# Six-layer decoder block on one core: GpSimd adds inputs and biases, VectorE makes some scan scalings, TensorE adds products of zeros

## What is computed

```
x = ln(x + L0_attn(x))    # hyena: x@w_in+b, short convolution, v*s1, long convolution, *s0, @w_out + b_out
x = ln(x + L0_xattn(x))   # softmax(x ctx^T/sqrt(d)) ctx (77 keys), its own layernorm * gamma + beta
x = ln(x + L0_ffn(x))     # quantised linear 128->512, gelu, quantised linear 512->128, + b2
x = ln(x + L1_attn(x))    # selective state-space scan, 256 channels, 16 states
x = ln(x + L1_xattn(x))   # 16-head cross attention with q/k norms, 77 keys, @Wo + bo
x = ln(x + L1_ffn(x))     # product-key mixture of 1024 experts, top 8 of 8 heads
```

## Time and profile before

| | us |
|---|---|
| median of 3 runs | 1079.09 |
| lowest, highest | 1075.49, 1084.47 |
| profiled execution, its own time | 1088.42 |
| its span, first to last instruction | 1086.6 |

### The profile page before, as it was taken

The page is one execution under the profiler, slowest core; times in us unless marked ns, Lnnn a source line. Parts: engine busy times, 40 slices in busy tenths (PEclk is TensorE's granted clock), DMA queues, the critical chain, the costliest instruction groups (busy, mean ns, idle before and its releaser), DMA issues.

```text
span 1086.6 us, 13799 instructions
## 1 busy us (share of the span) xinstructions
PE 816.7 (75%) x4536; PEld 591.9 (54%) x4536; DVE 768.4 (71%) x1635; ACT 697.3 (64%) x2068; POOL 298.3 (27%) x175
## 2 busy tenths in 40 slices
PE   1769485677898788988786775766688889988882
PEld 1547244566565546566555454455556664565562
DVE  1167845777755558899989677657865556999994
ACT  1423559997667665896754357678665777796660
POOL 3021102776455401000011213437554541000000
PEclk9888696988989888999999786789988999989997
DMA  8200001221100000000100001122210000000000
GB/s 239 60 1 2 0 25 49 78 78 59 49 1 1 1 0 1 18 1 1 27 1 10 1 22 30 40 60 76 71 39 1 0 1 1 1 1 1 1 1 21
DMA packets 27250, 29.06 MB, mean 27 GB/s; under 512 B 7220, under 2 KB 17194, under 8 KB 27178
## 3 DMA queue, kind: packets, MB, share of 16 engines
q1 hardware_dynamic: 25208, 26.20, 8.3%
q10 hardware_dynamic: 1970, 1.97, 0.6%
HBM read 26.33 MB, written 1.84 MB: 26 GB/s over the span
## 4 chain that ended last, share of the span: by engine, by line
DVE 35%; PE 30%; ACT 17%; issue 6%; POOL 6%; DMA 1%; POOLq 0%; DVEq 0%; ACTq 0%
DVE mem L1786 10%; ACT mem L1310 7%; POOL mem L1846 5%; DVE mem L1610 5%; DVE mem L1769 5%; ACT mem L1354 4%; PE ps L879 2%; PE ps L984 2%; PE ps L932 2%; PE ps L1105 2%; PE ps L1058 2%; DVE x L1414 2%; PE ps L846 2%; PE ps L888 1%; PE ps L1007 1%
## 5 line engine op out<-in xcount | busy, mean ns | idle before, releaser
L1826 POOL TENSOR_TENSOR rs<-ve,minus_half 128x4 f32<-128x4 f32 (+1 forms) x56 | 88.5, 1580 | 536.0 <-DVE ve L1407 422.2
L1610 DVE TENSOR_TENSOR_SCAN mem<-mem,ps 128x1024 f32<-128x1024 f32 x64 | 145.2, 2281 | 65.1 <-PE ps L879 64.8
L1846 POOL TENSOR_TENSOR mem<-mem 128x1024 f32<-128x1024 f32 x64 | 151.7, 2379 | 141.8 <-DVE mem L1610 129.0
L1105 PE MATMUL ps<-ident,mem 128*128 128x128 f32 x1024 | 140.6, 288 | 42.3 <-DVE mem L1786 37.8
L1786 DVE SCALAR_TENSOR_TENSOR mem<-mem 128x1024 f32<-128x1024 f32 x128 | 161.0, 1281 | 14.3 <-ACT mem L1354 11.8
L1354 ACT ACTIVATE mem<-mem 128x32 f32<-128x32 f32 x768 | 167.0, 314 | 3.7 <-PE ps L1105 3.7
L1105 PEld LDWEIGHTS ps<-ident,mem 128*128 128x128 f32 x1024 | 119.1, 148 | 82.5 <-DVE mem L1786 65.1
L1136 ACT ACTIVATE mem<-ps 128x1024 f32<-128x1024 f32 (+6 forms) x128 | 94.1, 748 | 108.2 <-PE ps L1058 52.5
L1310 ACT ACTIVATE mem<-ps,mem,rs 128x77 f32<-128x77 f32 x256 | 102.3, 437 | 45.3 <-DVE mem L1663 45.3
L1240 ACT ACTIVATE mem<-mem,m_A 128x511 f32<-128x511 f32 x128 | 84.1, 711 | 48.6 <-DVE mem L1610 46.6
L879 PE MATMUL ps<-ident,mem 128*128 128x128 f32 x512 | 79.3, 307 | 42.8 <-DVE mem L1610 26.4
(11 more groups left out here) (237 smaller groups left out, 1331.1 us busy)
## 6 DMA issues: line engine op xcount, KB each, us to landing
mem<-bc_rows SPq DMA_DIRECT2D x64, 256.0 KB, 3.3
mem<-in_x_dram SPq DMA_DIRECT2D x4, 256.0 KB, 3.0
mem<-key_rows SPq DMA_DIRECT2D x2, 512.0 KB
out_dram<-x SPq DMA_DIRECT2D x4, 256.0 KB, 2.3
mem<-in_mask_BxSxS_ik_dram SPq DMA_DIRECT2D x4, 154.0 KB, 3.1
mem<-n_L_ffn_expert_down_dram SPq DMA_DIRECT2D x1, 512.0 KB
mem<-in_L_xattn_Wo_dram SPq DMA_DIRECT2D x1, 512.0 KB
mem<-in_L_xattn_Wv_dram ACTq DMA_DIRECT2D x1, 512.0 KB
```

The costliest lines, as they stand in the source:

```text
L1105: mm = pe.matmul(ps[:, e // 4, (e % 4) * P:(e % 4 + 1) * P], WH[s][:, (k * PH + h) % WB, e * P:(e + 1) * P], ident[:], start=(h == 0 and e ...
L1610: nc.vector.tensor_tensor_scan((HS, TU)[n % 2][s][:].rearrange(flat), dA[s][:, n % 2].rearrange(flat), dbu.rearrange(flat), 0.0, ALU.mult, ...
L1846: nc.gpsimd.tensor_tensor(HC[s][:, n % 2], (HS, TU)[n % 2][s][:], spread(CQ[s][:, n % 2, :], 1, DJ), ALU.mult)\
```

## The change

- GpSimd gets four new additions per sample (`biased`): `R = input + bias` for `hyena`, `cross0`, `bitffn` and `cross1`. `added` becomes one float32 product of `ident` with `R`; in `cross0` and `bitffn` it goes altogether, with ScalarE's copy to `R2`, and VectorE reads `R` instead.
- In the scan VectorE makes `DZ` of four of the sixteen states of a lane (`VE_STATES`) as one `tensor_tensor` of 1024 elements (`DUT` times the spread column of `BT`), and ScalarE leaves those out.
- State 0's `DZ` is scaled straight out of PSUM; `DU` is transposed into banks 0 and 1 instead of 2 and 3; softplus' `Exp` and `Ln` come ahead of the copies of B and C, for both of which TensorE now waits.
- `zeros_added`: two bfloat16 products of a zero matrix with 512 columns are added onto bank 0 after the `DZ` transposes of each state from 2 on, and onto bank 3 after the scores of units 1 to 6 of the second cross attention. They change no sum.
- All five strings of `LANE_RUNS` are new. They start with lane 1.

```diff
+    VE_STATES = [(2, 6, 10, 14), (4, 8, 12, 15)]
...
-                def added(to, of, bias):
-                    pe.matmul(to, ident[:], of[:].rearrange("p k d -> p (k d)"), start=True, stop=False,
+                def added(s, to, turn_of):
+                    w.reach(G("xb_ready", s), turn_of)
+                    pe.matmul(to, ident[:], R[s][:].rearrange("p k d -> p (k d)"), start=True, stop=False,
                               skip_group_check=True)
-                    return pe.matmul(to, ident[:], spread(bias[:], 1, NB), start=False, stop=False,
-                                     skip_group_check=True)
+                def zeros_added(to, times, start=False):
+                    width = to.shape[1] // P
+                    for _ in range(times):
+                        pe.matmul(to, zeros_bf[:], spread(ident_bf[:], 1, width), start=start, stop=False,
+                                  skip_group_check=True)
...  (cross0, bitffn on TensorE)
-                    yield 3.1
-                    added(ps[:, 2, :], X[s], beta).then_inc(G("o_ready", s), 1)
-                    yield 4.5
-                    w.next(G("qT_ready", s), 2)
-                    added(ps[:, 1, :], X[s], b2).then_inc(G("v_ready", s), 1)
                     yield 5
-                    w.next(G("qT_ready", s), NB - 2)
+                    w.next(G("qT_ready", s), NB)
...  (scan on TensorE)
-                    w.next(G("bc_sb", s))
+                    w.next(G("bc_sb", s), 2)
-                            mm = pe.transpose(ps[:, 2 + k // 2, at:at + P], DU[s][:, j, k * P:(k + 1) * P], ident[:])
+                            mm = pe.transpose(ps[:, k // 2, at:at + P], DU[s][:, j, k * P:(k + 1) * P], ident[:])
...
                             mm.then_inc(G("dbu_done", s), 1)
+                            if n >= 2:
+                                zeros_added(ps[:, 0, :], 2)
                         if n >= 1:
                             yield (4.2, 4.8)[s] + n
+                            if n == 1:
+                                w.next(G("xT_ready", s))
...  (cross1 on TensorE)
+                        if 0 < u < 2 * NB - 1:
+                            zeros_added(ps[:, 3, :], 2)
-                    added(ps[:, 3, :], X[s], a_bo)
+                    added(s, ps[:, 3, :], 4)
...  (scan on ScalarE; Exp and Ln moved ahead of the two copies)
-                            turned(s, DUT[s][:].rearrange("p (a b) c -> p a (b c)", a=2), ps[:, 2:4, :], "xT_ready")
+                            w.next(G("turned", s))
+                            w.next(G("bc_sb", s), 2)
+                            for k in range(NB):
+                                ins = nc.scalar.activation(DZ[s][:, 0, k, :], ps[:, k // 2, k % 2 * DI:(k % 2 + 1) * DI],
+                                                           ACT.Identity, scale=BT[s][:, k, 0:1])
+                            ins.then_inc(G("dz_ready", s), 1)
+                            yield 3.5
+                            copy(DUT[s][:].rearrange("p (a b) c -> p a (b c)", a=2), ps[:, 0:2, :], G("xT_ready", s))
                             w.reach(G("xT_ready", s), XT_TURNS)
-                            w.next(G("bc_sb", s), 2)
+                            continue
+                        if n in VE_STATES[s]:
+                            continue
...  (scan on VectorE, after the recurrence of state n)
+                        if n + 2 in VE_STATES[s]:
+                            yield 4.3 + n
+                            w.reach(G("xT_ready", s), XT_TURNS)
+                            nc.vector.tensor_tensor(DZ[s][:, n % 2], DUT[s][:], spread(BT[s][:, :, n + 2], 2, DI),
+                                                    ALU.mult).then_inc(G("dzv_ready", s), 1)
...  (GpSimd)
+                def biased(s, of, bias):
+                    nc.gpsimd.tensor_tensor(R[s][:], of[:], spread(bias[:], 1, NB), ALU.add)\
+                        .then_inc(sg["xb_ready"][s], 1)
...
+                    yield 4000.2
+                    w.reach(sg["x_ready"][s], 4)
+                    biased(s, X[s], a_bo)
```

More of the change, by code:

```diff
@@ L1194, in bitffn @@
                                ps[:, k, :].bitcast(BF16)[:, 0:F], "qT_ready")
-                    yield 4.6
-                    w.reach(G("v_ready", s), len(GROUPS) + 1)
-                    copy(R2[s][:].rearrange("p k d -> p (k d)"), ps[:, 1, :], G("v_sb", s))
                 def scan(s, b):
@@ L1828, in rsqrt, with stages @@
                         .then_inc(sg["rstd_ready"][s], 1)
-                def stages(s):
-                    for stage in (4, 1003, 1004, 2000, 2003, 2005):
+                def biased(s, of, bias):
+                    nc.gpsimd.tensor_tensor(R[s][:], of[:], spread(bias[:], 1, NB), ALU.add)\
+                        .then_inc(sg["xb_ready"][s], 1)
+                def stages(s, b):
+                    yield 0.2
+                    if b >= 1:
+                        w.reach(sg["x_ready"][s], 0)
+                    w.next(sg["x_loaded"][s], 16)
+                    pool.wait_ge(p_late, ALL_LATE)
+                    biased(s, XI[s], b_out)
+                    yield 4
+                    rsqrt(s, P, NB)
+                    yield 4.6
+                    w.reach(sg["x_ready"][s], 1)
+                    biased(s, X[s], beta)
+                    for stage in (1003, 1004, 2000):
                         if stage == 1003:
@@ L1837, in stages @@
                                                     minus_half[0:C, 0:H], ALU.pow).then_inc(sg["krstd_ready"][s], 1)
+                        yield stage
+                        rsqrt(s, P, NB)
+                    yield 2000.1
+                    w.reach(sg["x_ready"][s], 2)
+                    biased(s, X[s], b2)
+                    for stage in (2003, 2005):
                         yield stage
@@ L1868, in program @@
                         w.batch(sg, TURNS, s, b)
-                        for stage in stages(s):
+                        for stage in stages(s, b):
                             yield PASS * b + clock(int(stage // 1000), stage % 1000)
```

57 lines of the change are left out of this document (31 added, 26 removed), and 39 rows, old and new, of tables (scalar, tensor, vector).

## The result

The changed kernel takes 1046.17 us, the median of 4 runs (1043.1 to 1047.16); the kernel before, run in turn with it, takes 1081.78. The ratio is 0.967 with an interval of [0.962, 0.973]: 35.6 us faster, where the prediction said 25 (1054 us, range 1016 to 1088). The profiled execution took 1047.16 us with a span of 1045.3. The same kernel was run once more beside later experiments.

The account below looks back on a forecast made before the run. No engine was full; the limit changed by stage, with ScalarE setting the pace where both lanes scan. Terms -9 - 3 - 3 + 0 - 10 = -25 took the median 1079 to 1054 us, range 1016 to 1088.

Parts of the forecast that it names:

- Scalings, -9: Where both lanes scan: moving scalings to VectorE brings 48 states from 3.03 to 2.85 us each, -9 us.
- Start of the scan, -3: State 0 no longer waits for the copy to `DUT`, and softplus starts earlier: -3 us (0 to -8).
- Additions, -3: Additions moved to GpSimd: `bitffn` gains 6 us, GpSimd's extra work costs 3, together -3 us (-6 to +13).
- The +3 for GpSimd: GpSimd's 16 additions stand ahead of reciprocal square roots and keep VectorE's two-input operations out: +3 us, from 0 to 19.
- Zeros, 0: Zero products in scans and cross attention: TensorE time costs +11 us, higher clock wins it back, 0 together (+11 to -20).
- The fourth rival: Zeros change no clock: +11 in place of 0, 1065 us; its chance lies inside the main forecast's 0.48.
- The third: Rival: zeros hold TensorE at 2.4 GHz, -18 in place of 0, 1036 us; chance 0.18 including larger gains of the strings.
- Strings, -10: New order runs the lanes closer: cover lost in pass 1, time won where a lane was alone; -10 us (-30 to +24).
- -35: Cross attention: five units a pass that ran alone save 3.5 us each, in two passes, -35 us.
- +24: Pass 1's first sublayers lose cover: VectorE's idle 20 of 114 us becomes pass 0's 44 of 124, +24 us.
- Closer lanes bringing nothing: Rival: lost cover costs 24 us, only 15 of 35 is won, +9 in place of -10, 1073 us; chance 0.20.
- The shared way to SBUF: Rival, scans: VectorE's idle time stays and each scaling adds 3.12 us, +37 in place of -9, 1100 us; chance 0.14.

Follow-up runs that it names:

- order-only kernel: The kernel before with only the five strings of `LANE_RUNS` replaced by the new ones: 1065.49 us against 1083.4, ratio 0.986 [0.981, 0.990].

## Why the prediction was right, and where its terms were off

The sign, the size class and the likeliest case were right: faster by 35.6 us, 25 forecast. The terms were less right than their sum: those of the strings and of the additions were too small by 8 and 5 us, and two of the others too large.

- **Scalings, -9.** The mechanism was right: ScalarE no longer leads, and recurrences came closer than said, 2.76 and 2.60 us apart instead of 2.85. Two parts of this term were mis-sized in the same direction: the scaling itself (1.53 instead of 1.7) and, above all, the waits between four engines near 2.6, which the forecast put at 0.25 a state and which were nearly nothing in pass 1. But the step from 3.03 was not all the scalings' doing: 2.86 to 2.92 came from the order alone. What the scalings brought is 8.7 us in the scans of the profiled executions and about 1 us, not told apart from 0, in the medians. That the -9 meets the 8.7 is chance: a greater drop a state than forecast, of which the order had a third to a half.
- **Start of the scan, -3.** 0.8 measured in the medians, not told apart from 0; in the profiled executions 3.3 in the scan of pass 0 and nothing in that of pass 1. That the other lane hides it there, the lower end that the term left open, is likely and not shown.
- **Additions, -3.** Measured -8. The -6 for `bitffn` held (2.7 and 1.0 us on the two lanes in pass 0). The +3 for GpSimd did not appear: its additions start when `x` is written, mostly on an idle GpSimd, and the square root behind one in pass 0 (101.17 us, changed kernel run again) came after 2.0 us of idle time. The rest, some 3 us, would be the products of the other sublayers, taken at 0; that is a difference and nothing shows it directly.
- **Zeros, 0.** The granted clock in the scans rose to 0.94 and 0.95, above the 0.93 named as the sign, and in the medians the net is within 3 us of nothing in the new order. The fourth rival (no change of the clock) fell. The third (-18 in place of 0) did not come either: zeros made scans and cross attentions some 7 us shorter, and longer experts took it back. The Trainium skill ("TensorE: Matmul & The Clock Gate", Part 4) says that transposes do not count as activity for the clock; the scans with no zeros ran only 27 of 143.9 and 20 of 139.5 us at the lower level. In the order-only kernel, all 339 TensorE products from 694.3 to 757.3 us are transposes, and the granted clock is 0.95. So this case doesn't bear it out; only that added zeros shortened the time at the lower level speaks for it.
- **Strings, -10.** This is the step that failed most. Measured: -18 in the medians and -22.9 in the profiled executions. By stage in the table: -11.4 and -4.1 in the scans, which the prediction had put to the scalings or nowhere; -23.3 and +6.8 in cross attention, -16.5 together where it said -35; +6.3 and +1.4 where it said +24 for lost cover. The +24 went wrong at a window. The prediction took VectorE's 44 idle us in 41 to 165 as what pass 1 would turn into. Of these, 19.8 lie ahead of the first new `x` (82.1 us; VectorE's first piece of the pass begins at 50.14, behind the loads), 12.5 in `cross0` and `bitffn`, and 11.9 behind 142, at the start of the scan. In pass 1 VectorE's idle time in the first three sublayers after is 16.5 us of 88.0, not the 44 that the prediction named as a sign; in the kernel before it is 24.9 of 89.8 at the same cuts. The 35 for cross attention was nearly all won in pass 0 (from first to last exponential 107.2 to 68.2 us after) and not in pass 1 (87.6 to 79.8), where the lanes lay closer together already. Units are 4.3 and 5.0 us apart in the mean, not 3.9, so the sign of more than 4 us a unit did appear (TensorE is busy 85 and 88% there). The three errors have different directions and partly cancel: 16 too much lost, 18 too much won, 15.5 in the scans left out.

The other rivals. Closer lanes bringing nothing (1073 us, 0.20) is refuted by the order-only kernel, 0.986 [0.981, 0.990]. The shared way to SBUF (1100 us, 0.14) named a true price, 2.9 us for each added scaling. The 16 as placed cost less than they save: put back on ScalarE, the scans are 8.7 us longer. (Its two thresholds don't go together: the 1.0 us a scaling counts 16 of them, the 2.3 for more than 1% slower only 12; by 16 that is (16 + 11)/16, or 1.7.) VectorE's idle time before the recurrences, 0.92 us a state in the earlier trace rows, is 0.65 with the order alone (14.2/22) and 0.1 after, so it was not the latency of a fixed chain, as the rival had it.

The single steps don't add up to 35.6: 18 (order), 8 (additions), 1 (scalings), 1 (start), -3 (zeros) are 25. That this is the forecast's own figure is chance. The order was laid out for the changed work, so its worth with that work may be larger than in the kernel before, and the kernel with both zeros and scalings undone lost more than the two did singly. How the remaining 11 us divide is open. A part of each number is also the state of the clock in the experts, below.

## What to carry to other kernels

When two lanes share the engines, price the order of the work as a part of the change, stage by stage, and cut the stages where a lane's data is written, not at round times: here a window that held the wait for loads put 24 us of loss on a stage that grew by 1.4. An engine that sets the pace by a fifth over the others (2.86 against 2.36 us a state) hides their floors; taking a quarter of one of its two jobs away moved the limit at once to two engines with no room left, where the next job of the same kind costs its full 2.9 us. And products of zeros that raise the clock have no price of their own: 9 us won in the kernel before, nothing or -3 in the new order, 13 once the experts had zeros too.

## What the runs showed of the hardware that was not expected

The experts of pass 0 come in two lengths with the same instructions in the same order there. In the profiled executions of the kernels in the new order with no zeros in the experts, the stage lasts 174.6 to 176.7 us with 24 to 26 us at the lower clock, or 181.1 to 182.4 with 34 to 41: some 0.35 us longer for each us at 1.2 GHz. The experts of pass 1 vary in the same way, 165.6 to 170.5 us. 182.4 us with 41 came in the changed kernel both times, in the one with state 0 scaled from the copy, and in one without any zeros; 24 came in kernels with zeros (each scaling twice, additions on TensorE) and in one without. So what stands ahead of the stage does not settle it in a way that these runs show. Executions of one kernel differ in the same manner: without zeros, three took 1040.8 to 1041.1 us at a mean granted clock of 0.888 and one 1048.2 at 0.879; the changed kernel run again took 1039.8 and 1046.2. The time up to the first new `x` of both lanes varies too, from 71.3 to 76.1 us in the new-order kernels' profiled executions. A step of 6 or 7 us between two versions of this kernel can be this and nothing else, which is why the undo of zeros, of scalings and of the scan's start are called unresolved above. What starts the longer spell at the lower clock stays open.

A recurrence of 1024 elements follows the last one after some 2.2 us when nothing is late, 0.08 less than its own listed duration, and the mean of GpSimd's products rises from 2.36 to 2.59 us, because each scaling on VectorE makes the product that meets it 3.24 to 3.37 us long. The floor of a state on GpSimd rose with the very work that was taken off ScalarE.
